# Empty edge slots and fill edges of a graph kernel read rows spread over the tables

## The chip, the cores and the metric

The kernel runs on one NeuronCore of a Trainium2 chip. Its engines work side by side, each through a queue of its own: PE (TensorE, matrix products), DVE (VectorE), ACT (ScalarE), POOL (GpSimd, which here issues the gathers) and SP (SyncE, which issues plain DMAs). Sixteen DMA engines move data between HBM and the on-chip memory SBUF. The metric is the device time of the whole kernel in microseconds.

## The reference, cut to what matters

Four layers run one after the other over one graph of 6250 nodes with 128 features and 100000 edges sorted by destination, each followed by a residual and a layer norm. What they do per edge:

```
L0 (twice):  agg[dst] += dinv[src] * w * dinv[dst] * h[src]
L1 (gat):    e = leaky(u[src] + v[dst]); agg[dst] += softmax_over_dst(e) * x[src]
L2 (hgt):    e = q[dst] . k[type][src];  agg[dst] += softmax_over_dst(e) * v[type][src]
L3:          e = relu(V [h[src], h[dst]]) + D h[src] + E h[dst]
             out[src] += scale * xw[dst] * e          (sums by src, self loops added)
```

## The kernel before, in words

**Slots.** Nodes are cut into NT = 49 tiles of P = 128. The kernel sorts the edges on the chip: each node tile gets a whole number of columns of 128 slots, and what is left of its last column stays empty. There are SC = 832 columns, 106496 slots for 100000 edges. One lane of a column is one partition. Tiles come in the order of their number of columns, and the last node tile comes last, so all columns that no tile needs stand at the very end of the order. There is one such order by destination (the d order) and one by source (the s order).

**Fill edges.** The input is laid out as 128 by UC = 784 entries, 352 more than there are edges. These 352 have src = dst = PAD_NODE = 6271, a node row that no real node has, and are sorted with the others; they stand at the end of the last tile's columns.

**What a slot reads.** `d_rec` in HBM holds one record of four numbers (src, dst key, typed row, weight) for each slot of the d order. Before the edges are scattered into it, DVE sets a buffer `fill` to zero with the key field at 1e6 (L400, L401) and SP copies it over `d_rec` (L364). ACT writes the edges' records, `d_recs`, from the sorted inputs (L370), and POOL scatters them (L721). So a slot that no edge takes keeps src = 0 and typed row = 0, and a fill edge has row 6271. The columns `d_src` and `d_typed` are read back from `d_rec`. For the s order, the tail of the second convolution decodes `s_dst` from a placing done with matrix products (`decoded`, L1365 to L1397); there an empty slot comes out as row 0 as well (L1391), and `dec_i` holds 256 for an empty slot and 0 for others (L1384).

**The five passes.** Each goes over all 832 columns in 104 groups of 8. For each column POOL issues one indirect DMA that fetches 128 table rows, one for each lane, at the row numbers in that column:

- c1: table t0 by `d_src`, rows of 512 B (L757); c2: table t1, the same
- gat: table t2 by `d_src`, 544 B; hgt: table t3 by `d_typed`, 1024 B
- L3: table t4 by `s_dst`, 1536 B (L2750)

Four group buffers are in use in turns (in L3 two, halved). In c1 and c2 PE waits for a group's landing (`landed`) and then multiplies the rows into the sums (L796). In gat and hgt DVE waits for it and scores (L2209, L2222), while ACT spills the rows to HBM; the weighing runs 12 groups behind. In L3 DVE waits for four columns at a time (L2836). A stage begins only when the last one is finished on all engines (`new_stage`).

Of the kernel before, what the change touches and what calls it, by code (L numbers as in the profile page):

```python
# [9 lines left out]
ALU = mybir.AluOpType  # L10
ACT = mybir.ActivationFunctionType
# [6 lines left out]
P = 128  # L18
NT = -(-N // P)
NP = NT * P  # L20
# [4 lines left out]
EC = P  # L25
UC = 784
UG = UC // 8
FULL_ROWS = E // EC
TAIL = E - FULL_ROWS * EC
# [3 lines left out]
SC = GROUPS * JC  # L33
# [10 lines left out]
SX = SC + 8 * (RING - 1)  # L44
BIG = 1.0e30
PAD_KEY = 1.0e6
HALF = (P - 1) / 2
EPS = 1e-5
AW = 35584
assert SC >= (UC * EC + NT * (P - 1)) // P and FULL_ROWS < UC and NG * GT == NT and UG % 2 == 0  # L50


# [24 lines left out]
def bcast_last(ap, n):  # L77
    shape = list(ap.shape) + [n]
    return ap.unsqueeze(len(shape) - 1).to_broadcast(shape)
# [6 lines left out]
def build(nc, t, out):  # L86
    ctx = ExitStack()
    with ctx:
# [21 lines left out]
        iota_part = sb("iota_part", 1)  # L110
# [34 lines left out]
        l3_T = sb("l3_T", 6 * D)  # L145
        arena = sb("arena", AW)

# [39 lines left out]
        e_in = {}  # L187
# [134 lines left out]
        d_recs = part(UC * 4).rearrange("p (c r) -> p c r", r=4)  # L322
# [9 lines left out]
        def hots(ap, keys, n, count):  # L332
# [10 lines left out]
        fill = part(JC * 16 * 4)  # L343
# [5 lines left out]
        tile_ge = part(SC)  # L349
        iota_c = part(SC)  # L350
        iota_ci = part(SC).bitcast(I32)
        split, filled, fill_set, iota_done, nodes, free, hist_done, base_v, base_p = (sem("h_" + n) for n in (
            "split", "filled", "fill_set", "iota_done", "nodes", "free", "done", "base_v", "base_p"))
        s_counts, d_counts = bank(0, 8 * NT), bank(1, NT)
        SIZED, PICKS = 3, 3
        with nc.Block() as block:
# [9 lines left out]

            @block.scalar
            def _(act):
                for f, n in enumerate(("src", "dst", "typ", "wgt")):
                    nc.scalar.activation(d_recs[:, :, f], e_in[n], ACT.Copy)  # L370

            @block.vector
            def _(dve):
                step = Chain(dve, split)
# [6 lines left out]
                for key, h, lo16, hi16 in ((e_in["src"], hi_int[0], s_lo16, s_hi16), (e_in["dst"], hi_int[1], d_lo16, d_hi16)):  # L381

                    step(nc.vector.tensor_scalar(h, key, -HALF, 1.0 / P, ALU.add, ALU.mult))
                    step(nc.vector.tensor_copy(hi16[:, 0:UC], h))
# [12 lines left out]
                for a in range(2):  # L397
                    step(nc.vector.tensor_tensor(w_rest, w_rest if a else e_in["wgt"], w_part[:, a], ALU.subtract))
                    step(nc.vector.tensor_copy(w_part[:, a + 1], w_rest))
                step(nc.vector.memset(fill, 0.0))  # L400
                nc.vector.memset(fill.rearrange("p (c r) -> p c r", r=4)[:, :, 1], PAD_KEY).then_inc(fill_set, 1)  # L401
                dve.wait_ge(iota_done, 1)
                step(nc.vector.tensor_copy(iota_c, iota_ci))
                dve.wait_ge(hist_done, 1)
                step = Chain(dve, base_v)
                step(nc.vector.tensor_copy(counts, d_counts))
# [841 lines left out]
        NODES_AT = 6144  # L1248
# [59 lines left out]
        class SecondNodes:  # L1308
# [9 lines left out]
            TAIL = 2 * (DONE + 1)  # L1318
# [47 lines left out]

            def decoded(self, dve, i):

                step = Chain(dve, self.d_v, (0, 3, 5, 6, 7, 8, 10, 12, 13, 13, 13)[i])
                if i == 0:  # L1370
                    step(nc.vector.tensor_scalar(small[:, 0:NT], s_degree, 1.0, None, ALU.add))
                    for z in range(2):
                        step(nc.vector.tensor_copy(dec_b[:, z * Q_W:(z + 1) * Q_W], place_bank(1, z)))
                elif i == 1:
                    for z in range(2):
                        step(nc.vector.tensor_copy(dec_a[:, z * Q_W:(z + 1) * Q_W], place_bank(0, z)))
                elif i == 2:
                    step(nc.vector.tensor_scalar(dec_int, dec_b, -HALF, 1.0 / P, ALU.add, ALU.mult))
                elif i == 3:
                    step(nc.vector.tensor_copy(dec_h, dec_int))  # L1380
                elif i == 4:
                    step(nc.vector.scalar_tensor_tensor(dec_b, dec_h, -float(P), dec_b, ALU.mult, ALU.add))
                elif i == 5:
                    step(nc.vector.tensor_scalar(dec_i, dec_a, 0.5, float(2 * P), ALU.is_lt, ALU.mult))  # L1384
                    step(nc.vector.tensor_tensor(s_lo[:, 0:SC], dec_b, dec_i, ALU.add))
                elif i == 6:
                    dve.wait_ge(self.d_deg, 1)
                    step(nc.vector.tensor_copy(deg_T, ps[0:NT, 3072:3072 + P]))
                    step(nc.vector.tensor_scalar(dec_a, dec_a, -1.0, 8.0, ALU.add, ALU.mult))
                elif i == 7:  # L1390
                    step(nc.vector.scalar_tensor_tensor(s_dst[:, 0:SC], dec_a, 0.0, dec_h, ALU.max, ALU.add))  # L1391
                elif i == 8:
                    dve.wait_ge(self.d_up, 1)
                    nc.vector.tensor_copy(dec_T.rearrange("p j e -> p (j e)"), ps[:, 2048:2048 + 7 * P]).then_inc(self.d_sb, 1)
                elif i == 9:
                    dve.wait_ge(self.d_deg, 2)
                    nc.vector.tensor_copy(inv[:, :], ps[:, 3584:3584 + NT])  # L1397
# [112 lines left out]
            def tensor_tail(self, pe):  # L1510
                for s in range(self.TAIL, self.TAIL + self.STEPS):
                    self.tensor_step(pe, s, self.in_tail(s, (0, 1, 2, 7, 8, 9)))
                    if s == self.TAIL + 4:
                        pe.wait_ge(self.d_v, 5)
                        nc.tensor.transpose(ps[0:NT, 3072:3072 + P], small[:, 0:NT], ident[:, :]).then_inc(self.d_deg, 1)
                        nc.tensor.matmul(ps[:, 2048 + 6 * P:2048 + 7 * P], ident[:, :], ident[:, :], start=True, stop=True)
                    if s == self.TAIL + 6:
                        pe.wait_ge(self.d_v, 10)
                        for j, k in BLOCKS:
                            last = nc.tensor.transpose(ps[0:k, 2048 + j * P:2048 + (j + 1) * P], s_lo[:, j * P:j * P + k], ident[:, :])  # L1520
                        last.then_inc(self.d_up, 1)
                    if s == self.TAIL + 7:
                        pe.wait_ge(self.d_v, 11)
                        nc.tensor.matmul(ps[:, 3584:3584 + NT], deg_T, rank_hot, start=True, stop=True).then_inc(self.d_deg, 1)

            def tensor_step(self, pe, s, todo):
# [38 lines left out]
        dec_a, dec_b, dec_h, dec_i = (arena[:, i * SC:(i + 1) * SC] for i in range(4))  # L1565
        dec_int = dec_i.bitcast(I32)
        dec_T = arena[:, 4 * SC:4 * SC + 7 * P].rearrange("p (j e) -> p j e", j=7)
        deg_T = arena[0:NT, 4 * SC + 7 * P:4 * SC + 8 * P]
        assert 4 * SC + 8 * P <= NODES_AT
        convolve("c1", t0, 0, FirstNodes)  # L1570
        convolve("c2", t1, 1, SecondNodes)

        class ThirdNodes:
# [8 lines left out]
            FIRST_HALF, TAIL, STEPS = 24, 2 * DONE, 5  # L1582
# [936 lines left out]
        r, x_new, summed_a = (scratch(AT_Q + i * GC, GC) for i in range(3))  # L2519
# [412 lines left out]
```

## Time and profile before

| | us |
|---|---|
| runs | 7548.39, 7556.19, 7559.97 (median 7556.19) |
| profiled execution | 7554.35, its span 7552.5 |
| POOL busy | 4883.0 (65%) |
| PE busy | 4910.9 (65%) |
| DVE busy | 4682.7 (62%) |
| ACT busy | 3188.4 (42%) |
| DMA | 925.24 MB, mean 123 GB/s |

No engine is busy all the time; the stages differ, and each has to be read by itself. The span leaves 1.85 us of the profiled execution outside. In the rows below, a row of the order of time gives start, duration, engine, line and operation; the brackets give the idle time of the engine just before it and what ended that.

### The profile page before, as it was taken

To read this page: it belongs to the slowest core of one execution; us is meant where nothing else is said; L and a number is where in the kernel's file an instruction comes from. 1 tells how busy PE (TensorE), PEld (TensorE's weight loads), DVE (VectorE), ACT (ScalarE), POOL (GpSimd) and SP (SyncE) were. 2 spreads that over 40 slices of the span, in tenths; PEclk is the share of its full clock that TensorE was granted. 3 is DMA by queue.
4 is the path that set the end of the run, shared out by engine and by line. 5 is a ranking of instruction groups with operands and counts; after the bars stand their busy time and mean duration, and the time that the engine had idled before them with its cause. 6 is when DMAs were issued, how large, how long until landed. Compare 5 with 4: busy or idle time off the path is not lost. (4 is left out here: it accounts for less than half of the span.)

```text
span 7552.5 us, 95692 instructions
## 1 busy us (share of the span) xinstructions
PE 4910.9 (65%) x26906; PEld 3728.8 (49%) x26906; DVE 4682.7 (62%) x12437; ACT 3188.4 (42%) x7393; POOL 4883.0 (65%) x4968
## 2 busy tenths in 40 slices
PE   8999801666676777774365655856656666777774
PEld 6777601444444455553254544435555543555553
DVE  8999801555554577775456666645666566566666
ACT  0222200444443444442244444746665642555553
POOL 0677775777776777774777773047777700777774
PEclk9776655888887888886566666967887787899997
DMA  1333201222223222223666665567777822766665
GB/s 29 79 82 79 58 2 28 52 55 55 56 55 48 53 56 55 56 55 56 168 180 183 183 183 118 195 196 230 231 230 224 221 69 82 217 209 210 209 208 146
DMA packets 817681, 925.24 MB, mean 123 GB/s; under 512 B 120147, under 2 KB 656219, under 8 KB 816923
## 3 DMA queue, kind: packets, MB, share of 16 engines
q0 software_dynamic: 198144, 441.54, 23.4%
q1 hardware_dynamic: 395118, 365.43, 16.2%
q10 hardware_dynamic: 223916, 112.15, 5.1%
q8 instruction: 245, 4.01, 0.2%
q14 instruction: 258, 2.11, 0.1%
HBM read 724.85 MB, written 193.87 MB: 122 GB/s over the span
## 5 line engine op out<-in xcount | busy, mean ns | idle before, releaser
L757 POOL DMA_INDIRECT arena<-t,d_src x2496 | 2441.0, 978 | 902.6 <-issue 759.2
L796 PE MATMUL ps<-arena 128*128 128x128 f32 (+2 forms) x8320 | 1779.4, 374 | 755.9 <-DMA arena<-t,d_src 623.5
L796 PEld LDWEIGHTS ps<-arena 128*128 128x128 f32 x8320 | 1567.2, 255 | 1015.7 <-issue 921.6
L805 DVE TENSOR_TENSOR arena<-arena,ps 128x512 f32 (+2 forms) x1040 | 835.4, 803 | 710.4 <-PE ps L796 656.9
L757 POOL DMA_INDIRECT arena<-t,d_typed x832 | 817.2, 982 | 488.8 <-issue 252.7
L721 POOL DMA_INDIRECT d_rec<-arena x784 | 789.0, 1006 | 442.7 <-issue 251.9
L2750 POOL DMA_INDIRECT arena<-t,s_dst x832 | 795.5, 956 | 295.6 <-issue 250.7
L793 PE MATMUL ps<-int_tmp 128*128 128x512 bf16 (+1 forms) x1664 | 554.7, 402 | 475.0 <-DVE arena L805 238.9
L1234 PE MATMUL ps<-arena 128*128 128x416 f16 x3328 | 770.4, 385 | 0.0
L1975 PE MATMUL ps<-arena 128*128 x2496 | 408.5, 296 | 451.7 <-ACT arena L1870 294.2
L1173 ACT ACTIVATE arena<-arena 128x128 f16<-128x128 f16 x1664 | 662.6, 480 | 6.9
L1975 PEld LDWEIGHTS ps<-arena 128*128 128x128 f32 (+1 forms) x2496 | 352.4, 204 | 518.9 <-issue 493.3
L1875 ACT ACTIVATE arena<-iota_row,d_lw 128x128 f32<-128x128 f32 x1664 | 506.5, 387 | 211.6 <-DMA arena<-t,d_src 167.6
L1193 DVE TENSOR_SCALAR arena<-iota_row,d_lw 128x128 f32<-128x128 f32 x1664 | 473.2, 360 | 79.4 <-DVE x_cur L1425 31.9
L1234 PEld LDWEIGHTS ps<-arena 128*128 128x128 f16 x3328 | 334.8, 114 | 249.7 <-issue 103.0
L1168 ACT ACTIVATE arena<-iota_row,arena 128x128 f16<-128x128 f32 x832 | 264.5, 391 | 426.3 <-PE ps L1236 409.5
L793 PEld LDWEIGHTS ps<-int_tmp 128*128 128x128 bf16 x1664 | 154.4, 110 | 581.6 <-DVE arena L805 308.8
L2779 ACT ACTIVATE arena<-iota_row,s_lo 128x128 f32<-128x128 f32 x832 | 254.4, 388 | 430.3 <-PE ps L796 430.3
L2836 DVE TENSOR_TENSOR ps<-ps,arena 128x512 f32<-128x512 f32 x208 | 145.3, 699 | 423.8 <-DMA arena<-t,s_dst 369.8
L2222 DVE TENSOR_TENSOR arena<-ps,arena 128x512 f32<-128x512 f32 x208 | 135.2, 687 | 404.0 <-DMA arena<-t,d_typed 357.6
L1202 DVE TENSOR_SCALAR arena<-arena 128x832 f16<-128x832 f16 x832 | 316.8, 442 | 0.0
L683 PEld LDWEIGHTS ps<-arena 128*128 128x128 f32 x1568 | 258.8, 254 | 53.1 <-issue 45.3
(451 smaller groups left out, 8054.2 us busy)
## 6 DMA issues: line engine op xcount, KB each, us to landing
spill<-arena ACTq DMA_DIRECT2D x208, 512.0 KB, 4.2
arena<-spill SPq DMA_DIRECT2D x208, 512.0 KB, 5.1
arena<-d_loT SPq DMA_DIRECT2D x208, 256.0 KB, 5.0
arena<-s_loT SPq DMA_DIRECT2D x104, 512.0 KB, 4.9
arena<-key_d SPq DMA_DIRECT2D x98, 512.0 KB
t<-arena SPq DMA_DIRECT2D x49, 1024.0 KB, 4.4
arena<-t,d_src POOLq DMA_INDIRECT x2496
arena<-t,d_typed POOLq DMA_INDIRECT x832
```

What stands on the lines that cost most here:

```text
L721: pool.indirect_dma_start(out=d_rec[:, :], out_offset=bass.IndirectOffsetOnAxis(ap=row[:, c:c + 1], axis=0), in_=d_recs[:, c, :], in_offse ...
L757: pool.indirect_dma_start(out=rows[r][:, i, :], out_offset=None, in_=table, in_offset=bass.IndirectOffsetOnAxis(ap=idx[:, 8 * n + i:8 * n ...
L793: nc.tensor.matmul(half[:, :, 0:self.width], zeros16[:, 0:P], self.blank, start=True, stop=False, skip_group_check=True)
L796: return nc.tensor.matmul(self.banks[i // 4][:, bass.ds(self.slot[i], self.width)], weights, rows, start=False, stop=False, skip_group_che ...
L805: nc.vector.tensor_tensor(at, at, got, ALU.add).then_inc(self.added, 1)
L1173: last = nc.scalar.activation(at_r[:, b, a, j], far[:, b, j], ACT.Relu, bias=places[:, 2 + 2 * a, at_c + j:at_c + j + 1], scale=places[:, ...
L1193: one_hot = nc.vector.tensor_scalar(at[:, s, :], iota_row[:, :], lw[:, 8 * n + i, 0:1], lw[:, 8 * n + i, 1:2], ALU.is_equal, ALU.mult)
L1202: nc.vector.tensor_scalar(at_q[:, b, j], iota_q, places[:, 0, at_c + j:at_c + j + 1], None, ALU.is_equal)
L1234: nc.tensor.matmul(place_bank(a, z), at_r[:, b, a, j], at_q[:, b, j, z * Q_W:(z + 1) * Q_W], start=False, stop=False, skip_group_check=True)
L1875: last = nc.scalar.activation(at[:, b, i], iota_row[:, :], ACT.Abs, bias=lw[:, 8 * n + i, 0:1], scale=-1.0)
L1975: last = nc.tensor.matmul(looked_up(b, z)[:, (i - 4 * z) * tab_w:(i - 4 * z + 1) * tab_w], hot_T[:, b, i * P:(i + 1) * P], source[:, bass. ...
L2750: pool.indirect_dma_start(out=rows[:, 8 * b + i, :], out_offset=None, in_=t4, in_offset=bass.IndirectOffsetOnAxis(ap=s_dst[:, 8 * n + i:8 ...
```

## The change

An empty slot and a fill edge are given row numbers that differ from slot to slot. In the d order, the empty record's src and typed row become 7 times the slot's position modulo 832 (0 to 5817); the fill edges' src and typed row become 49 times their lane (0 to 6223). In the s order an empty slot's row becomes 49 times its lane; the fill edges' `s_dst` stays at 6271. The keys stay, so where an edge goes and what is summed stay too.

```diff
+SPREAD, LANE_SPREAD = 7, 49
@@ first sorting stage, ACT
+                for f in (0, 2):
+                    nc.scalar.activation(d_recs[:, FULL_ROWS:UC, f], iota_part[:, 0:1].to_broadcast([P, UC - FULL_ROWS]), ACT.Copy, scale=float(LANE_SPREAD)).then_inc(pads_set, 1)
                 for f, n in enumerate(("src", "dst", "typ", "wgt")):
-                    nc.scalar.activation(d_recs[:, :, f], e_in[n], ACT.Copy)
+                    if n in ("src", "typ"):
+                        nc.scalar.activation(d_recs[:, 0:FULL_ROWS, f], e_in[n][:, 0:FULL_ROWS], ACT.Copy)
+                        act.wait_ge(pads_set, 2)
+                        nc.scalar.activation(d_recs[0:TAIL, FULL_ROWS, f:f + 1], e_in[n][0:TAIL, FULL_ROWS:FULL_ROWS + 1], ACT.Copy)
+                    else:
+                        nc.scalar.activation(d_recs[:, :, f], e_in[n], ACT.Copy)
@@ first sorting stage, DVE
-                step(nc.vector.memset(fill, 0.0))
-                nc.vector.memset(fill.rearrange("p (c r) -> p c r", r=4)[:, :, 1], PAD_KEY).then_inc(fill_set, 1)
                 dve.wait_ge(iota_done, 1)
                 step(nc.vector.tensor_copy(iota_c, iota_ci))
+                fields = fill.rearrange("p (c r) -> p c r", r=4)
+                step(nc.vector.memset(fill, 0.0))
+                step(nc.vector.memset(fields[:, :, 1], PAD_KEY))
+                nc.vector.tensor_scalar(fields[:, :, 0:4:2], bcast_last(iota_c, 2), float(SPREAD), None, ALU.mult).then_inc(fill_set, 1)
@@ tail of the second convolution, DVE (the counts of d_v that others wait for go up by one or two)
                 if i == 0:
                     step(nc.vector.tensor_scalar(small[:, 0:NT], s_degree, 1.0, None, ALU.add))
+                    step(nc.vector.tensor_scalar(spread, iota_part[:, 0:1], LANE_SPREAD / (2 * P), None, ALU.mult))
@@
                 elif i == 7:
+                    step(nc.vector.scalar_tensor_tensor(dec_h, dec_i, spread, dec_h, ALU.mult, ALU.add))
                     step(nc.vector.scalar_tensor_tensor(s_dst[:, 0:SC], dec_a, 0.0, dec_h, ALU.max, ALU.add))
```

On DVE, in the first sorting stage, before (L400 and L401 set `fill`, L403 makes `iota_c`, L406 reads the first counts):

```order
L399 CAST arena<-arena 128x784
L400 MEMSET arena 128x3328
L401 MEMSET arena 128x832
L403 CAST arena<-arena 128x832
L406 COPY arena<-ps 128x49
```

and now:

```order
L408 CAST arena<-arena 128x784
L410 CAST arena<-arena 128x832
L412 MEMSET arena 128x3328
L413 MEMSET arena 128x832
L414 TENSOR_SCALAR arena<-arena 128x1664
L417 COPY arena<-ps 128x49
```

The making of `iota_c` stands ahead of the two memsets now, and a TENSOR_SCALAR over 1664 elements stands behind them, ahead of the counts.

On DVE, in the tail of the second convolution, the last steps of the decoding, before:

```order
L1450 TENSOR_SCALAR arena<-x_cur,arena 128x128 x4
L1465 TENSOR_TENSOR arena<-arena,bias_sb 128x512
L1466 TENSOR_TENSOR arena<-arena,bias_sb 128x512
L1391 SCALAR_TENSOR_TENSOR s_dst<-arena 128x832
L1394 COPY arena<-ps 128x896
```

and now:

```order
L1463 TENSOR_SCALAR arena<-x_cur,arena 128x128 x4
L1478 TENSOR_TENSOR arena<-arena,bias_sb 128x512
L1479 TENSOR_TENSOR arena<-arena,bias_sb 128x512
L1403 SCALAR_TENSOR_TENSOR arena<-arena 128x832
L1404 SCALAR_TENSOR_TENSOR s_dst<-arena 128x832
L1407 COPY arena<-ps 128x896
```

One more pass over 832 elements stands directly ahead of the one that writes `s_dst`.

## Rows read from the trace of the kernel before

**Rows 1.** the costliest groups: line, engine, operation, count | busy us, mean ns | idle, releasers

```profile
L757 POOL DMA_INDIRECT arena<-t,d_src x2496 | 2441.0, 978 | 902.6 <-issue 759.2
...
L2750 POOL DMA_INDIRECT arena<-t,s_dst x832 | 795.5, 956 | 295.6 <-issue 250.7
```

**Rows 2.** stretches: us; PE, PEld, DVE, ACT, POOL busy (instructions); PEclk, DMA share, GB/s

```profile
2320.00:2360.00 40.00, 26.89 (x152) 18.48 (x152) 21.91 (x66) 18.98 (x52) 30.56 (x32) 0.87 0.22 57
2376.00:2404.00 28.00, 16.30 (x78) 12.07 (x79) 9.70 (x28) 4.46 (x12) 12.05 (x13) 0.74 0.85 36
5980.00:6010.00 30.00, 16.62 (x103) 14.83 (x102) 21.72 (x40) 14.13 (x33) 23.30 (x23) 0.73 0.71 212
6033.00:6061.00 28.00, 12.69 (x72) 11.70 (x72) 10.05 (x16) 12.37 (x25) 10.70 (x11) 0.68 1.00 109
```

**Rows 3.** order of time, end of c1, POOL and PE

```profile
2350.07 0.94 POOL L757 DMA_INDIRECT arena<-t,d_src  x1 [0.30 <-issue]
...
2352.66 1.15 PE L796 MATMUL ps<-arena 128*128 128x128 f32 x8 [3.02 <-DMA arena<-t,d_src]
...
2389.86 2.07 PE L796 MATMUL ps<-arena 128*128 128x128 f32 x8 [5.46 <-DMA arena<-t,d_src]
...
2390.76 0.94 POOL L757 DMA_INDIRECT arena<-t,d_src  x1 [0.30 <-issue]
...
2403.57 1.64 PE L796 MATMUL ps<-arena 128*128 128x128 f32 x6 [5.70 <-DMA arena<-t,d_src]
```

**Rows 4.** order of time, end of c2, POOL and PE

```profile
3479.81 0.95 POOL L757 DMA_INDIRECT arena<-t,d_src  x1 [0.30 <-issue]
...
3492.06 2.07 PE L796 MATMUL ps<-arena 128*128 128x128 f32 x8 [4.39 <-DMA arena<-t,d_src]
```

**Rows 5.** order of time, end of gat, POOL and DVE

```profile
4588.47 0.94 POOL L757 DMA_INDIRECT arena<-t,d_src  x1 [0.30 <-issue]
...
4592.18 0.36 DVE L2209 TENSOR_REDUCE arena<-ps 128x64 f32<-128x192 f32 x1 [6.40 <-DMA arena<-t,d_src]
...
4619.44 0.95 POOL L757 DMA_INDIRECT arena<-t,d_src  x1 [0.30 <-issue]
...
4637.06 0.36 DVE L2209 TENSOR_REDUCE arena<-ps 128x64 f32<-128x192 f32 x1 [6.30 <-DMA arena<-t,d_src]
```

**Rows 6.** order of time, end of hgt, POOL and DVE

```profile
5985.20 0.95 POOL L757 DMA_INDIRECT arena<-t,d_typed  x1 [0.30 <-issue]
...
5989.94 1.29 DVE L2222 TENSOR_TENSOR arena<-ps,arena 128x512 f32<-128x512 f32 x2 [3.38 <-DMA arena<-t,d_typed]
...
6045.92 0.95 POOL L757 DMA_INDIRECT arena<-t,d_typed  x1 [0.30 <-issue]
...
6063.61 1.29 DVE L2222 TENSOR_TENSOR arena<-ps,arena 128x512 f32<-128x512 f32 x2 [8.75 <-DMA arena<-t,d_typed]
```

**Rows 7.** order of time, end of L3's pass, POOL and DVE

```profile
7438.86 0.96 POOL L2750 DMA_INDIRECT arena<-t,s_dst  x1 [0.30 <-issue]
...
7442.28 0.70 DVE L2836 TENSOR_TENSOR ps<-ps,arena 128x512 f32<-128x512 f32 x1 [0.51 <-DMA arena<-t,s_dst]
...
7469.10 0.96 POOL L2750 DMA_INDIRECT arena<-t,s_dst  x1 [0.30 <-issue]
...
7481.90 0.70 DVE L2836 TENSOR_TENSOR ps<-ps,arena 128x512 f32<-128x512 f32 x1 [3.47 <-DMA arena<-t,s_dst]
```

**Rows 8.** order of time, first sorting stage and the next one's start, DVE and ACT

```profile
173.52 0.75 DVE L401 MEMSET arena<- 128x832 f32 x1 [0.83 <-DVE arena L400]
...
200.97 0.92 ACT L560 ACTIVATE arena<-arena 128x392 bf16<-128x392 bf16 x1 [168.65 <-DVE arena L334]
```

**Rows 9.** order of time, tail of c2, DVE

```profile
3529.24 0.59 DVE L1389 TENSOR_SCALAR arena<-arena 128x832 f32<-128x832 f32 x1
...
3533.38 1.02 DVE L1391 SCALAR_TENSOR_TENSOR s_dst<-arena 128x832 int32<-128x832 f32 x1
...
3538.91 0.69 DVE L1472 TENSOR_TENSOR arena<-ps,bias_sb 128x512 f32<-128x512 f32 x1 [3.38 <-PE ps L1543]
```

More of the change, by code:

```diff
@@ L49 @@
 AW = 35584
+assert SPREAD * (SC - 1) < NP and LANE_SPREAD * (P - 1) < NP and EC == P and TAIL % 32 == 0
 assert SC >= (UC * EC + NT * (P - 1)) // P and FULL_ROWS < UC and NG * GT == NT and UG % 2 == 0
@@ L351, in build @@
         iota_ci = part(SC).bitcast(I32)
-        split, filled, fill_set, iota_done, nodes, free, hist_done, base_v, base_p = (sem("h_" + n) for n in (
-            "split", "filled", "fill_set", "iota_done", "nodes", "free", "done", "base_v", "base_p"))
+        split, filled, fill_set, pads_set, iota_done, nodes, free, hist_done, base_v, base_p = (sem("h_" + n) for n in (
+            "split", "filled", "fill_set", "pads_set", "iota_done", "nodes", "free", "done", "base_v", "base_p"))
         s_counts, d_counts = bank(0, 8 * NT), bank(1, NT)
@@ L1367, in decoded @@
             def decoded(self, dve, i):
-                step = Chain(dve, self.d_v, (0, 3, 5, 6, 7, 8, 10, 12, 13, 13, 13)[i])
+                step = Chain(dve, self.d_v, (0, 4, 6, 7, 8, 9, 11, 13, 15, 15, 15)[i])
                 if i == 0:
                     step(nc.vector.tensor_scalar(small[:, 0:NT], s_degree, 1.0, None, ALU.add))
+                    step(nc.vector.tensor_scalar(spread, iota_part[:, 0:1], LANE_SPREAD / (2 * P), None, ALU.mult))
                     for z in range(2):
@@ L1513, in tensor_tail @@
                     if s == self.TAIL + 4:
-                        pe.wait_ge(self.d_v, 5)
+                        pe.wait_ge(self.d_v, 6)
                         nc.tensor.transpose(ps[0:NT, 3072:3072 + P], small[:, 0:NT], ident[:, :]).then_inc(self.d_deg, 1)
@@ L1517, in tensor_tail @@
                     if s == self.TAIL + 6:
-                        pe.wait_ge(self.d_v, 10)
+                        pe.wait_ge(self.d_v, 11)
                         for j, k in BLOCKS:
@@ L1522, in tensor_tail @@
                     if s == self.TAIL + 7:
-                        pe.wait_ge(self.d_v, 11)
+                        pe.wait_ge(self.d_v, 12)
                         nc.tensor.matmul(ps[:, 3584:3584 + NT], deg_T, rank_hot, start=True, stop=True).then_inc(self.d_deg, 1)
@@ L1568, in build @@
         deg_T = arena[0:NT, 4 * SC + 7 * P:4 * SC + 8 * P]
-        assert 4 * SC + 8 * P <= NODES_AT
+        spread = arena[:, 4 * SC + 8 * P:4 * SC + 8 * P + 1]
+        assert 4 * SC + 8 * P + 1 <= NODES_AT
         convolve("c1", t0, 0, FirstNodes)
```

## The prediction, made before the changed kernel ran

> **What bounds the kernel now.** I read the costliest groups first. POOL issues 832 gathers in each of five passes; one takes about 0.98 us and 0.3 us of idle time that the profile puts down to nothing but issue [rows 1]. So a pass lasts at least 832 columns by some 1.27 us, and inside a pass PE or DVE wait for landings, never the reverse: POOL's idle time ahead of a gather is 0.30 us to the last one [rows 3 to 7]. The change takes no gather away, so it can't shorten this part.
>
> The second view is the table of stretches, for what the DMA engines do near the end of a pass [rows 2]. In c1 they are busy 22% and move 57 GB/s from 2320 to 2360 us. From 2376 to 2404 they are busy 85% and move only 36 GB/s. In hgt they go from 71% and 212 GB/s to 100% and 109 GB/s. More time for fewer bytes: in these last microseconds each row has become dear. The input says which columns those are. Counted from the reference's inputs, the d order fills 809 of 832 columns and the s order 810, so the last 23 (22) are empty and all their 128 lanes read row 0; the 352 fill edges before them are 2.75 columns that all read row 6271.
>
> The third view is the order of time there. Gathers go in groups of 8, group 99 (columns 792 to 799) being the last before the fill edges and group 103 the last of all. In c1 group 99's last issue ends at 2350.07 + 0.94 = 2351.01 and PE starts on it at 2352.66, 1.65 us later; group 103's ends at 2391.70 and PE starts at 2403.57, 11.87 us later [rows 3]. The last two groups land 2403.57 - 2389.86 = 13.71 us apart, 1.71 us for a column or 13.4 ns for a row, where POOL takes (2390.76 - 2350.07) / 32 = 1.27 us for a column. A column of one row is thus slower to fetch than to issue, by 0.44 us; 25.75 such columns make 11.4 us, near the measured growth of 11.87 - 1.65 = 10.22. After this last landing come only products, sums and stores, then the next stage: this lag is on the path.
>
> **The change part by part.**
>
> *The lag at the end of each pass.* It goes if spread rows are fetched faster than POOL issues them, as random rows are in mid-pass at 22% (c1) or 71% (hgt) of the DMA engines [rows 2]. I take the wait of a normal group for the wait that stays.
> - c1: 11.87 - 1.65 = 10.2 us [rows 3].
> - c2: last issue ends 3480.76, PE starts 3492.06: 11.3; the table has the same row size, so c1's normal 1.65 holds: 9.7 us [rows 4].
> - gat: last issue ends 4620.39, DVE scores at 4637.06: 16.7. Group 100 took 4592.18 - 4589.41 = 2.8 [rows 5], with two columns of fill edges in it; taken as normal, 13.9 us. With c1's 1.65 it would be 15.0.
> - hgt: 6063.61 - 6046.87 = 16.7, normal 5989.94 - 5986.15 = 3.8: 12.9 us [rows 6].
> - L3: 7481.90 - 7470.06 = 11.8, normal 7442.28 - 7439.82 = 2.5, for half groups: 9.3 us [rows 7]. Its fill edges keep row 6271; 2.75 columns by 0.4 us are 1.2 us of lag, which the 22 columns behind them make up.
>
> The sum is 56.0 us. Is each on the path? PE waited 5.7 us for c1's last landing and 4.4 for c2's [rows 3, 4]; of c1's 13.71 us between landings, 8.0 were work, and that fits into POOL's 10.2 us for a group. In gat and hgt DVE idled 6.3 and 8.8 us ahead of the last score, so it keeps up too, also if landings come 3 or 4 us closer together; behind it the weighing of 12 groups follows in program order, no sooner and no later than before [rows 5, 6]. In L3 DVE idled 3.5 us ahead of the last four columns [rows 7].
>
> *Empty slots inside used columns.* Each tile's last column has on average 65 of them. At 13.4 ns they cost 0.87 us, under the 1.27 us of issue, so they delay nothing that POOL's pace doesn't cover: zero, now and after.
>
> *First sorting stage, DVE.* A TENSOR_SCALAR of 1664 elements is added on DVE's chain: `iota_c` and the counts follow one on the other, without a wait for another engine. 832 elements took 0.59 us in that operation and 1.02 us in one with two inputs [rows 9]; twice as many lie between 1.0 and 1.9 us (estimates by doubling less the fixed part). The second memset is now waited for, and behind such a wait stood 0.83 us [rows 8]; between 0 and 0.8. Sum +1.0 to +2.7, I take +2.0. The copy of `fill` starts as much later, and hides: the stage ends at about 200 us, 26 us behind the memset [rows 8].
> By the Trainium skill (VectorE: DVE Perf Modes, Mode 2×_2P) an fp32 operation with one tensor input can run at two elements a cycle. The 0.59 us row agrees. With it this addition would be at the low end, and the forecast 1 us lower, which a measurement of this kernel can't show.
>
> *First sorting stage, ACT.* Two small ACTIVATEs and two tails of one column come in. ACT's next work after this stage follows 168.65 us of idle time [rows 8]: zero. Without that cover they would cost some 1 us.
>
> *Tail of c2, DVE.* The pass over 832 elements ahead of `s_dst` takes 1.02 us like its neighbour [rows 9]. DVE idles 3.38 us for PE shortly behind it, which covers it: zero, 1.0 if not. The small operation for `spread` is on the chain there, +0.2.
>
> The sum: -56.0 + 2.0 + 0.2 = -53.8 us. On the profiled execution, 7554.35, that gives 7500.5; it lay 1.8 us under the median of the runs, 7556.19, so the median should be **7502**.
>
> **The rivals.**
>
> *Spread rows are served only half better.* The new rows aren't random: 7 rows apart from lane to lane in the d order, 49 apart in the s order, and there the same 128 rows in all 22 columns. If a column then takes 1.5 us in place of 1.71, half of the lag stays: 7556 - 28 + 2 = 7530. Against it: the same DMA engines serve random rows in a fraction of the time. For it: no row of before shows a regular step. 12%.
>
> *The gain in gat and hgt meets the next limit.* If PE, DVE or the spill's way out and back takes over half of their 26.8 us: 7502 + 13 = 7515. For it: the DMA engines are at 71% there in mid-pass, and the weighing waits for reloads. Against: the idle times above. 12%.
>
> *Not the row.* The lag might come from something else at a pass's end, and the spreading then does nothing: 7556 + 2 = 7558. Against it: issue, size and count of the gathers are the same in group 99 and group 103; what differs is what the row numbers say. 5%.
>
> *Slower.* A regular step could send all lanes to one part of the memory and be worse than one row. The place is the same last 22 to 23 columns. Were a column to take 3.4 us, twice today's, the lag of a pass would be (3.4 - 1.27) by 23 = 49 us in place of 10, and five passes would add about 195 us: 7750. It is slower than before once a column takes over 1.71 us, and by over 0.2% from about 1.84 (15 us over five passes of 23 columns). Nothing in the trace speaks for it. 3%.
> The Trainium skill (DMA: Bandwidth & Descriptors, Latency and other measured facts) has such a loss, to half the rate, for HBM row pitches of large powers of two up to several MiB. [...]
>
> **How the numbers follow.** Chances: forecast 68% (7488 to 7520), half served 12%, next limit 12%, not the row 5%, slower 3%. If no lag at all were left, the sum would be -68 + 2, or 7490, so 7488 is the low end, with a microsecond or two for the runs' own scatter. The high end takes in the half-served case: 7530. That leaves out about 1 in 10 and the tails. About 0.2%, 15 us, is what a measurement of this kernel can tell from no change: faster needs under 7541, which the first three cases give, less a little for a poorly served one: 89%. Within 0.2%: 8%. Slower: 3%.
>
> **What would show it.** In the changed profile: the last PE start of c1 and c2 1.5 to 3 us behind POOL's last issue, DVE's last score 2 to 5 us behind it in gat and hgt, and 2 to 4 in L3; DMA share in the last 28 us of c1 near 22%, not 85%; each pass's POOL time unchanged; the first sorting stage 1 to 3 us longer. The prediction is wrong if landings in the last group still come 13 us apart, or if they come at POOL's pace and the stage ends no sooner.

## The result, and the profile after

| | us |
|---|---|
| before, runs beside it | median 7554.81 (7546.55 to 7559.97, 6 runs) |
| changed kernel | median 7495.75 (7485.98 to 7500.12, 6 runs) |
| ratio | 0.9922, 95% interval 0.9909 to 0.9935 |
| profiled execution | 7495.48, its span 7493.7 |

The change saves 59 us, 0.8%. The span of the profiled execution fell by 58.8, from 7552.5. (Two sets of later runs were some 16% slower for every kernel, the one before included; their totals are compared only within their set, and they are called runs at the slow pace.)

First the stretches, as in [rows 2]. Columns: us; busy time of PE, PEld, DVE, ACT, POOL with instruction counts; PE's granted clock; DMA share; GB/s. Here c1's last 28 us are 2367 to 2395.

```profile
2320.00:2360.00 40.00, 27.14 (x147) 19.18 (x146) 20.65 (x63) 18.66 (x50) 30.53 (x31) 0.84 0.21 55
2367.00:2395.00 28.00, 20.87 (x112) 14.48 (x110) 15.44 (x44) 9.82 (x27) 21.29 (x23) 0.82 0.19 51
...
6000.00:6020.00 20.00, 11.37 (x73) 10.23 (x71) 10.64 (x17) 13.12 (x32) 10.67 (x11) 0.82 0.66 196
```

The end of c1 now looks like its middle. The DMA engines are busy 19% where they were busy 85%, and move 51 GB/s where they moved 36. In hgt 66% and 196 GB/s stand against 100% and 109.

Then the order of time at the ends of the passes, which answers to [rows 3 to 7]. c1:

```profile
2386.93 1.19 PE L807 MATMUL ps<-arena 128*128 128x128 f32 x8 [3.09 <-DMA arena<-t,d_src]
...
2394.51 0.94 POOL L768 DMA_INDIRECT arena<-t,d_src  x1 [0.30 <-issue]
...
2397.10 1.15 PE L807 MATMUL ps<-arena 128*128 128x128 f32 x8 [3.03 <-DMA arena<-t,d_src]
...
2410.17 0.94 POOL L768 DMA_INDIRECT arena<-t,d_src  x1 [14.71 <-POOLq L103]
```

POOL's last issue ends at 2395.45 and PE starts on that group at 2397.10, 1.65 us later, exactly what a normal group took before [rows 3]; it was 11.87. The last two groups start 10.17 us apart, which is POOL's pace for 8 columns, no longer 13.71. The next pass's first gather waits 14.71 us; in the trace of before that bracket is 25.51.

c2, gat, hgt and L3:

```profile
3473.26 0.94 POOL L768 DMA_INDIRECT arena<-t,d_src  x1 [0.30 <-issue]
...
3475.89 1.29 PE L807 MATMUL ps<-arena 128*128 128x128 f32 x8 [2.87 <-DMA arena<-t,d_src]
```

```profile
4601.78 0.95 POOL L768 DMA_INDIRECT arena<-t,d_src  x1 [0.30 <-issue]
...
4605.94 0.36 DVE L2223 TENSOR_REDUCE arena<-ps 128x64 f32<-128x192 f32 x1 [3.76 <-DMA arena<-t,d_src]
...
6012.76 0.95 POOL L768 DMA_INDIRECT arena<-t,d_typed  x1 [0.30 <-issue]
...
6015.59 1.29 DVE L2236 TENSOR_TENSOR arena<-ps,arena 128x512 f32<-128x512 f32 x2 [4.90 <-DMA arena<-t,d_typed]
...
7419.08 0.70 DVE L2850 TENSOR_TENSOR ps<-ps,arena 128x512 f32<-128x512 f32 x1 [1.94 <-DMA arena<-t,s_dst]
...
7420.98 0.96 POOL L2764 DMA_INDIRECT arena<-t,s_dst  x1 [0.30 <-issue]
...
7424.10 0.70 DVE L2850 TENSOR_TENSOR ps<-ps,arena 128x512 f32<-128x512 f32 x1 [1.86 <-DMA arena<-t,s_dst]
```

The lags are 1.7, 3.2, 1.9 and 2.2 us where they were 11.3, 16.7, 16.7 and 11.8. POOL's pace is what it was: its groups of gathers have the same mean and the same idle time for issue as in [rows 1], and only the idle time between passes is less (881.1 where 902.6 stood, for the three passes by `d_src`):

```profile
L768 POOL DMA_INDIRECT arena<-t,d_src x2496 | 2441.7, 978 | 881.1 <-issue 759.5 <-POOLq L103 121.7
```

Here is where the span went. The table cuts it into the five passes, each from POOL's first gather to the end of its last issue, and the gaps between, from the start and end times of those rows:

| us | before | after | difference |
|---|---|---|---|
| start to c1's first gather | 1325.52 | 1328.83 | +3.31 |
| the five passes, issue time | 5327.85 | 5326.56 | -1.29 |
| gap behind c1 | 25.51 | 14.71 | -10.80 |
| gap behind c2 | 68.54 | 58.07 | -10.47 |
| gap behind gat | 356.03 | 342.20 | -13.83 |
| gap behind hgt | 366.61 | 351.56 | -15.05 |
| from L3's last issue to the end | 82.49 | 71.74 | -10.75 |

The five gaps give 60.9 us; with the other two rows 58.9, the whole change of the span.

### The profile page after: what moved, and what is told of

It reads as the page before. It is cut to its first block and busy times, and to the rows that moved or that the text cites. A ratio compares the mean times of both kernels' runs of the same rounds, so it can differ in the third digit from the quotient of the medians.

```text
span 7493.7 us, 95699 instructions
## 1 busy us (share of the span) xinstructions
PE 4880.7 (65%) x26906; PEld 3706.3 (49%) x26906; DVE 4683.1 (62%) x12440; ACT 3189.1 (43%) x7397; POOL 4882.0 (65%) x4968
## 5 line engine op out<-in xcount | busy, mean ns | idle before, releaser
L768 POOL DMA_INDIRECT arena<-t,d_src x2496 | 2441.7, 978 | 881.1 <-issue 759.5
```

The lines of the kernel that those rows point to most:

```text
L768: pool.indirect_dma_start(out=rows[r][:, i, :], out_offset=None, in_=table, in_offset=bass.IndirectOffsetOnAxis(ap=idx[:, 8 * n + i:8 * n ...
```

## Experiments

The first four ran side by side (before: 7570.64, the median of 25 runs). The gaps given with them are of their profiled executions.

**Zero steps.** The changed kernel with all its instructions and both steps at 0: does the gain come from the row numbers?

```diff
-SPREAD, LANE_SPREAD = 7, 49
+SPREAD, LANE_SPREAD = 0, 0
```

> The changed kernel with both steps set to 0: every instruction of the change is there, but empty slots and fill edges read row 0 again. Theory (the row numbers alone make the gain): the end of c1 lags again by 10 us (PE starts 11.9 us behind POOL's last issue, not 1.65), the gap between POOL's last gather of a pass and the first of the next is that of the kernel before in all four places (25.5, 68.5, 356 and 367 us, within 1), and the whole takes what the kernel before takes plus 1 to 3 us, so a ratio of 1.0001 to 1.0004. Rival (the moved steps or where they stand make part of the gain): the ratio is clearly under 1, near 0.992 if all of it.

Measured: 7573.68, ratio 1.0006 (0.9996 to 1.0015). Every gap is back (26.85, 70.86, 356.71, 368.99, 83.02 us), though three of the first four are 1.3 to 2.4 us longer than before's, where within 1 was expected. The end of c1 in its trace:

```profile
2390.01 0.94 POOL L768 DMA_INDIRECT arena<-t,d_src  x1 [0.30 <-issue]
2390.45 2.07 PE L807 MATMUL ps<-arena 128*128 128x128 f32 x8 [6.22 <-DMA arena<-t,d_src]
...
2403.98 2.07 PE L807 MATMUL ps<-arena 128*128 128x128 f32 x8 [6.38 <-DMA arena<-t,d_src]
```

The lag is 2403.98 - 2390.95 = 13.0 us, and the groups are again 13.5 us apart. The row numbers alone make the whole gain; the added instructions cost nothing that can be measured. The lag is 1.2 us longer than before's 11.87. What differs from before is that the fill edges now read row 0 too, not a row of their own; that is also the likely reason for the longer gaps.

**The d order alone, the s order alone.** In the first the step of the decoding is 0; in the second `SPREAD` and the step of the fill edges are.

```diff
-  step(nc.vector.tensor_scalar(spread, iota_part[:, 0:1], LANE_SPREAD / (2 * P), None, ALU.mult))
+  step(nc.vector.tensor_scalar(spread, iota_part[:, 0:1], 0.0, None, ALU.mult))
```

> Rows are spread in the d order alone (passes c1, c2, gat, hgt); an empty slot of the s order reads row 0, since the decoding multiplies by 0. Theory: each pass carries its own lag, so L3's comes back in full (about 10 us) and the four others stay away: 7496 + 10 = 7506 us, ratio 0.9935. DVE's last landing in L3 again 11.8 us behind POOL's last issue. Rival (the lags hang together, an earlier pass's end feeds the next): L3's lag differs from 11.8 us by over 1 us.

Measured: 7514.63, ratio 0.9931 (0.9915 to 0.9948), some 52 us, where 0.9935 was expected. Four gaps are within 1.2 us of those of after (14.39, 58.28, 342.68, 350.43), and L3's is that of before, 82.68. Its last gather and score show the 11.75 us:

```profile
7413.07 0.96 POOL L2764 DMA_INDIRECT arena<-t,s_dst  x1 [0.30 <-issue]
7419.07 0.70 DVE L2850 TENSOR_TENSOR ps<-ps,arena 128x512 f32<-128x512 f32 x1 [3.57 <-DMA arena<-t,s_dst]
7425.78 0.70 DVE L2850 TENSOR_TENSOR ps<-ps,arena 128x512 f32<-128x512 f32 x1 [3.55 <-DMA arena<-t,s_dst]
```

The last two scores, each of which waited for its four columns, are 6.71 us apart here, 1.68 a column; in the changed kernel 5.02, 1.26.

```diff
-SPREAD, LANE_SPREAD = 7, 49
+SPREAD, LANE_SPREAD = 0, 49
-  nc.scalar.activation(d_recs[:, FULL_ROWS:UC, f], ..., ACT.Copy, scale=float(LANE_SPREAD))
+  nc.scalar.activation(d_recs[:, FULL_ROWS:UC, f], ..., ACT.Copy, scale=0.0)
```

> Rows are spread in the s order alone (pass L3); empty slots and fill edges of the d order read row 0. Theory: L3's gain alone, about 10 us, less 1 to 3 us of added steps: 7548 us, ratio 0.9990. The four gaps of the d passes are as in the kernel before within 1 us. Rival: with spread rows at L3's place alone the gain is near 0, since something else takes over there.

Measured: 7566.52, ratio 0.9996 (0.9986 to 1.0005). L3's last gap is 71.43, 11.1 us less than before, and the last score follows 2.1 us behind the last issue, as in the changed kernel. But the other four gaps are longer than before's by 1.3, 2.3, 0.5 and 3.0 us, where within 1 was expected. The first experiment has the same, and in both the d order's fill edges read row 0. 7.1 of the 11.1 us are lost so and 4.0 remain; the medians differ by 4.1, but the interval of the ratio takes in 1, so the total shows no gain by itself. The expected ratio was 0.9990. That each order's spreading acts on its own passes is shown; the total is not a clean sum of parts, because what the fill edges read moves it.

**Fill edges alone.** They keep their spread rows, all empty slots read row 0: how much of the lag is the fill edges'?

```diff
-SPREAD, LANE_SPREAD = 7, 49
+SPREAD, LANE_SPREAD = 0, 49
-  step(nc.vector.tensor_scalar(spread, iota_part[:, 0:1], LANE_SPREAD / (2 * P), None, ALU.mult))
+  step(nc.vector.tensor_scalar(spread, iota_part[:, 0:1], 0.0, None, ALU.mult))
```

> Only the 352 fill edges of the d order are spread (2.75 columns); the 23 empty columns behind them read row 0, in both orders. Theory (each column of one row adds its own 0.44 us of lag): each d pass ends 1.2 us earlier than with all in one row, so PE starts 10.7 us behind POOL's last issue in c1 in place of 11.9, and the whole gains some 5 us less the added 1 to 3: about 7552. Rival (the fill edges alone start a jam that the empty columns only carry on): over 3 us less lag in each pass.

Measured: 7570.95, ratio 1.0002 (0.9991 to 1.0012).

```profile
2405.59 2.07 PE L807 MATMUL ps<-arena 128*128 128x128 f32 x8 [5.94 <-DMA arena<-t,d_src]
...
2419.61 0.95 POOL L768 DMA_INDIRECT arena<-t,d_src  x1 [25.72 <-POOLq L103]
```

The last issue ended at 2419.61 - 25.72 = 2393.89, so c1's lag is 11.70 us, before's within 0.2. The expected 1.2 us less did not come. So there are three cases of c1's lag: fill edges on row 0 with the empty slots, 13.03; on a row of their own, 11.87; spread, 11.70. Only the first adds to the lag. By the price of 0.44 us a column over POOL's pace, 23 columns make 10.1 us and 25.75 make 11.3; above the normal 1.65 the trace has 10.2 in before and 11.4 with zero steps. Columns of another row add nothing to the lag at the end, then, where columns of row 0 follow. The next runs ask what makes a row dear.

**One row, two rows, many rows, in a whole pass.** Three kernels made from the one before, at the slow pace (before there: 8722.16, a single run). The columns of `d_src`, `d_typed` and `s_dst` are not used as row numbers; each pass reads for all its columns one fixed column `pick`, row number lane // (128 / k) * step. `PICKS_OF` gives k (how many different rows) and step for c1, c2, gat, hgt and L3, in this order for the first, second and third kernel. So the sums are not the reference's; sizes, counts and issue are.

```diff
-  in_offset=bass.IndirectOffsetOnAxis(ap=idx[:, 8 * n + i:8 * n + i + 1], axis=0)
+  in_offset=bass.IndirectOffsetOnAxis(ap=pick[:, gather_pass[0] - 1:gather_pass[0]], axis=0)
+PICKS_OF = [(1, 0), (2, 1), (4, 1), (1, 0), (1, 0)]
+PICKS_OF = [(8, 1), (2, 1000), (1, 0), (2, 1), (2, 1)]
+PICKS_OF = [(128, 1), (128, 32), (128, 49), (128, 256), (128, 1)]
```

> The kernel before, but every gather of a pass reads a fixed set of rows, in place of its edges' rows (so the results mean nothing): in c1 all 128 lanes read row 0; in c2 half of the lanes row 0 and half row 1; in gat four neighbouring rows, 32 lanes each; in hgt and L3 row 0 for all. Theory (fetches of one row are served one after the other at some 13.4 ns, whatever its size up to 1536 B): c1 takes 832 x 1.71 = 1423 us from first to last landing where it took 1078; hgt 832 x 1.75 = about 1460; L3 832 x 1.66 = about 1380. In c2 with two rows, if the rows are served side by side, 0.86 us for a column, under POOL's 1.27: c2 as before (1064 us of issue), and gat too. Rival (it is the number of bytes or the pass's end that matters): c1 stays at 1066. Second rival (neighbouring rows share what is slow): c2 is as slow as c1.

> As the run with fixed rows in every pass: in c1 eight neighbouring rows of 512 B, 16 lanes each; in c2 two rows 1000 apart (512000 B); in gat row 0 (544 B) for all; in hgt rows 0 and 1 (1024 B); in L3 rows 0 and 1 (1536 B). Theory: c1 at POOL's pace, 1066 us; c2 with two rows at POOL's pace like its neighbouring pair in the other run; gat 832 x 1.75 = about 1460 us; hgt and L3 at POOL's pace (1070 and 1057) if two rows are served side by side. Rival (what is shared is a larger piece of memory than a row): two neighbouring rows are as slow as one, two distant rows are not.

> As the runs with fixed rows in every pass, but 128 different rows: in c1 neighbours (512 B apart), in c2 32 rows apart (16 KiB), in gat 49 rows apart (26656 B), in hgt 256 rows apart (256 KiB), in L3 neighbours (1536 B apart). Theory (different rows, whatever their step, are served faster than POOL issues): all five at POOL's pace, 1066, 1064, 1071, 1070 and 1057 us of issue. Rival (a step of a power of two sends all lanes to one part of the memory, up to half the rate or worse): c2 or hgt longer by over 5%, hgt most.

Measured: 9475.19, 9052.18 and 8739.78 (a single run each). Stretches inside c1, hgt and L3 of the three kernels, and inside gat of the last two; columns: us, POOL busy with its instructions, PE's clock, DMA share, GB/s. The first kernel (one row in c1, four in gat, one in hgt, one in L3):

```profile
1700.00:2500.00 800.00, 456.97 (x476) 0.75 0.92 42
...
6100.00:6900.00 800.00, 386.32 (x392) 0.67 0.94 143
8100.00:8600.00 500.00, 272.63 (x286) 0.80 0.99 150
```

The second (eight rows, one, two, two):

```profile
1700.00:2500.00 800.00, 537.91 (x554) 0.74 0.17 49
...
4500.00:5300.00 800.00, 396.08 (x405) 0.60 0.97 118
6100.00:6900.00 800.00, 467.30 (x474) 0.69 0.61 170
8100.00:8600.00 500.00, 330.00 (x346) 0.82 0.56 182
```

The third (128 rows in each):

```profile
1700.00:2500.00 800.00, 535.14 (x552) 0.73 0.17 49
...
4500.00:5300.00 800.00, 477.60 (x487) 0.63 0.51 143
6100.00:6900.00 800.00, 475.15 (x478) 0.70 0.60 176
8100.00:8600.00 500.00, 330.92 (x346) 0.80 0.60 182
```

Read the gathers in a stretch: with one row 476, 405, 392 and 286; with two or more 552 to 554, 485 to 487, 474 to 478 and 346. With one row the DMA engines are busy 92 to 99%, otherwise 17 to 61%. Two rows in a column are enough, next to each other or, in c2, 1000 rows apart (546 gathers in 800 us both times, 545 with 128 rows). More rows gain little on two: in hgt the issue of the whole pass took 1398.3 us with two rows and 1372.7 with 128, 2% less, and L3 took 1203.8 both times. A step of 32 rows in c2 (16 KiB) and of 256 rows in hgt (256 KiB) costs nothing: in c2 the DMA engines are busy 16%, where neighbouring rows in c1 have 17%. This takes away the rival in which a regular step would be slow, for these two steps.

One limit of these runs: at the slow pace a column of c1 and c2 takes 1.46 us and not 1.27, so that two rows keep up with POOL's normal pace isn't shown by them; the last experiment takes that up. They also show that it is not the bytes that make a row dear: one row of 544 B in gat took 1652.9 us for the pass, 1.99 a column, and one row of 1024 B in hgt 1662.7, 2.00. Both passes have the spill beside them.

**Empty slots alone, and the change again.** Is the fill edges' part worth anything? The first of the pair leaves out all that the change does to `d_recs` on ACT; the second is the changed kernel. Both ran at the slow pace (before there: 8777.33, 19 runs).

```diff
-  for f in (0, 2):
-      nc.scalar.activation(d_recs[:, FULL_ROWS:UC, f], iota_part[:, 0:1].to_broadcast(...), ACT.Copy, scale=float(LANE_SPREAD)).then_inc(pads_set, 1)
...
+      nc.scalar.activation(d_recs[:, :, f], e_in[n], ACT.Copy)
```

> The change without its ACT part: empty slots are spread in both orders, the 352 fill edges keep row 6271. Theory (the empty columns at the very end make the lag; what the fill edges' 2.75 columns add is made up behind them): the same time as the whole change, within 0.1% of it, about 7496 on a chip where the kernel before takes 7555, ratio 0.992; the ends of c1 and c2 lag as in the changed kernel, within 0.3 us. Rival (each column of one row adds its own 0.44 us for good, as my sum of 25.75 columns had it): 1.2 us more in each of four passes, so 5 us slower than the whole change.

> The changed kernel again, beside the one without the fill edges' part and on the same chip. Both theories: ratio 0.992 to the kernel before. It is there to say how much of a difference between the two is their own, and whether the 2.7 us by which the stages before c1 were longer in its first profile come back (if they do, the added steps cost more than the 0.6 us read at the first sorting stage; if not, they were scatter).

Measured: 8759.58, ratio 0.9987 (0.9967 to 1.0008), and 8782.78, ratio 0.9996 (0.9979 to 1.0014). Neither differs from before here, and the pair tells nothing of the fill edges. That the change itself gains nothing here was not expected. The trace of the second kernel shows who sets the pace. PE's products with the rows, in the changed kernel at the normal pace and in this run:

```profile
L807 PE MATMUL ps<-arena 128*128 128x128 f32 (+2 forms) x8320 | 1762.7, 372 | 743.6 <-DMA arena<-t,d_src 611.7
```

```profile
L807 PE MATMUL ps<-arena 128*128 128x128 f32 (+2 forms) x8320 | 1782.7, 365 | 445.3 <-issue 388.1
```

One product takes as long as ever (365 ns, 372). But where PE idled for landings, it now idles between products for nothing that the profile shows. In c1 it waits for a landing twice, where it did so 104 times at the normal pace; DVE in gat and hgt does so at most twice, where it was 88 and 80 times. Only in L3 does DVE still wait for landings, up to the last one. The end of c1:

```profile
2692.51 0.37 PE L807 MATMUL ps<-arena 128*128 128x128 f32 x1 [1.80 <-issue]
...
2697.74 0.94 POOL L768 DMA_INDIRECT arena<-t,d_src  x1 [0.30 <-issue]
...
2710.47 1.05 PE L807 MATMUL ps<-arena 128*128 128x128 f32 x8
```

PE takes up the last group 11.8 us behind POOL's last issue, with no wait ahead of it, although no row is dear in this kernel: it is still busy with earlier groups. POOL waits for buffers in turn, and c1's issue takes 1214.3 us, 1.46 a column. Rows that land 10 us late would find PE busy there, so that the lag of c1 and c2, and likewise that of gat and hgt, would be hidden; L3's 10 us are 0.1%, which the interval still allows. This is argued from the changed kernel alone: no profile of the kernel before was taken at that pace. What PE's added idle times are is open.

**One row a column.** Are two rows served side by side when they stand in different gathers? Again fixed columns in place of the row numbers, so the sums are not the reference's. c1: row 0 always. c2 and hgt: columns of row 0 and of row 1 in turns. L3: groups of eight columns of row 0 and of row 1000 in turns. gat: 128 rows, step 49. At the slow pace, beside the pair above.

```diff
+        def chosen(which, n, i):
+            c = (0, (0, 1)[i % 2], 3, (0, 1)[i % 2], (0, 2)[n % 2])[which]
+            return pick[:, c:c + 1]
-  in_offset=bass.IndirectOffsetOnAxis(ap=idx[:, 8 * n + i:8 * n + i + 1], axis=0)
+  in_offset=bass.IndirectOffsetOnAxis(ap=chosen(gather_pass[0] - 1, n, i), axis=0)
```

> The kernel before with fixed rows for every gather (the results mean nothing): c1 reads row 0 in all lanes of all columns; c2 and hgt read row 0 in even columns and row 1 in odd ones, all 128 lanes of a column the same row; gat reads 128 rows, 49 apart; L3 reads row 0 for the 8 columns of a group and row 1000 for the next 8. Theory (one row's fetches queue up behind each other, two rows are served side by side, also if they belong to different gathers in flight): c2 goes at POOL's pace like gat, c1 at 1.13 or more times POOL's pace, hgt at the pace it had with two rows. Rival (a gather is slow when its own 128 rows are one): c2 and hgt as slow as c1 with one row. L3: by the theory as slow as one row where only one group is in flight, between the two if several are.

Measured: 8960.43 (a single run).

```profile
1700.00:2500.00 800.00, 457.92 (x476) 0.75 0.97 42
3100.00:3900.00 800.00, 523.16 (x540) 0.79 0.44 48
...
6100.00:6900.00 800.00, 475.44 (x477) 0.69 0.69 177
8100.00:8600.00 500.00, 328.54 (x344) 0.85 0.89 180
```

With row 0 always, 476 gathers in 800 us; with two rows in turns 540, 477 and (in 500 us) 344, where the changed kernel beside it has 540, 478 and 342. So two rows are served side by side also from different gathers, even where eight columns of the one follow eight of the other. That fits the fill edges on row 6271, which added nothing to the lag at the end: their columns could be fetched beside those of row 0.

**Empty slots alone, once more,** at the normal pace (before: 7551.14, 7 runs); the edit is that of the pair.

> The change without its ACT part once more, since the first comparison ran where every kernel took 16% longer and told nothing. Theory (the fill edges' 2.75 columns are made up behind them): as the whole change, ratio 0.992, ends of c1 and c2 within 0.3 us of the changed kernel's (PE's last rows 2.98 and 3.20 us behind POOL). Rival (each column of one row counts for good): 1.2 us more lag in each of four passes, 0.993.

Measured: 7490.8, ratio 0.9922 (0.9905 to 0.9938), the ratio of the whole change. The gaps are those of after (14.76, 58.23, 341.70, 349.84, 71.65), and PE starts on the last group 1.60 (c1) and 1.73 us (c2) behind POOL's last issue, within 0.3 us of after's 1.65 and 1.69, as expected. The spreading of the d order's fill edges contributes nothing that can be measured. They have a lag of their own, though. Group 100, which holds most of their columns, and the next one, in c1:

```profile
2355.82 0.94 POOL L761 DMA_INDIRECT arena<-t,d_src  x1 [0.30 <-issue]
...
2359.68 2.07 PE L800 MATMUL ps<-arena 128*128 128x128 f32 x8 [4.28 <-DMA arena<-t,d_src]
...
2366.07 0.94 POOL L761 DMA_INDIRECT arena<-t,d_src  x1 [0.30 <-issue]
...
2368.62 1.33 PE L800 MATMUL ps<-arena 128*128 128x128 f32 x8 [2.06 <-DMA arena<-t,d_src]
```

PE starts on group 100 2.92 us behind its last issue and on group 101 1.61 us behind: 1.3 us of lag, made up within one group.

**One row at the normal pace.** Row 0 in every column of c1, hgt and L3; c2 in turns; gat 128 rows. Is the price of a one-row column the same when POOL is quicker?

```diff
-            c = (0, (0, 1)[i % 2], 3, (0, 1)[i % 2], (0, 2)[n % 2])[which]
+            c = (0, (0, 1)[i % 2], 3, 0, 0)[which]
```

> The kernel before with fixed rows for every gather (the results mean nothing): c1 (512 B rows), hgt (1024 B) and L3 (1536 B) read row 0 for every lane of every column; c2 reads row 0 in even and row 1 in odd columns, gat 128 rows 49 apart. Theory (12.8 to 13.4 ns for each fetch of one row, whatever its size): c1 issues for 1362 to 1423 us where it took 1066, L3 for 1380 to 1452 where it took 1057, c2 and gat at POOL's pace (1064, 1071). hgt took 2.0 us a column where the chip was slower: between 1.7 and 2.0, 1420 to 1660. Rival (the 16% slower chip made its own price): a price clearly under 12.8 ns here.

Measured: 8838.18 (a single run). Stretches in c1, c2, hgt and L3, columns as in [rows 2]:

```profile
1500.00:2500.00 1000.00, 568.47 (x2840) 423.47 (x2839) 422.26 (x1235) 342.12 (x925) 574.64 (x599) 0.75 1.00 42
2800.00:3800.00 1000.00, 739.70 (x4199) 546.57 (x4198) 745.06 (x2583) 477.90 (x1425) 763.32 (x777) 0.83 0.51 55
5400.00:6400.00 1000.00, 410.38 (x2306) 371.82 (x2306) 378.69 (x658) 376.72 (x758) 487.95 (x496) 0.68 0.98 144
7600.00:8600.00 1000.00, 645.30 (x2560) 469.07 (x2558) 443.04 (x568) 411.64 (x782) 544.30 (x571) 0.80 0.88 150
```

From its first gather to its last issue c1 takes 1361.49 us, where the first fixed-row kernel took 1361.28 at the slow pace. So the price belongs to the fetching, not to the issue. Per column it is 1.64 us in c1 (512 B rows), 1.98 in hgt (1024 B, with the spill beside it) and 1.75 in L3 (1536 B), from issue times of 1361.5, 1651.5 and 1453.8: 12.8, 15.5 and 13.7 ns a row. The expected price, 12.8 to 13.4 ns, holds for c1 and nearly for L3; hgt's 1651.5 us is inside its own expected range. c2, in turns, runs near POOL's pace, 1070.3 us against before's 1063.5; the other profiles at this pace have 1063.3 to 1065.1, so one row a column in turns costs some 6 us here. And POOL now waits inside c1, for buffers that PE hands on late.

## Why the prediction was right, point by point

**The bound.** POOL's pace held: 5326.6 us of issue in five passes against 5327.8. Nothing inside a pass got faster.

**The lag.** The forecast took 56.0 us off the five lags; the gaps shrank by 60.9. c1 was to give 10.2 and gave 10.8, c2 9.7 and 10.5, gat 13.9 and 13.8, hgt 12.9 and 15.1, L3 9.3 and 10.8. "The wait of a normal group is the wait that stays" was exact in c1 and c2 (1.65 and 1.69), near in gat (3.2 for 2.8) and L3 (2.2 for 2.5), and mis-sized in hgt: 1.9 for 3.8. That one term is 2 of the 5 us that were missed; 3 more stand behind the lag.

**What stands behind the lag.** The forecast let products, sums and stores after the last landing be as they were. They got shorter. From PE's last start behind a landing to the next pass's first gather, the four profiles at the normal pace that have the lag in c1 took 13.6 to 14.0 us, and the three without it 12.8 to 13.2; for c2 it is 57.0 to 57.9 against 56.4 to 56.6. From L3's last score to the end it is 70.6 to 71.4 against 69.4 to 69.6. That is 0.6, 0.9 and 1.1 us between before and after; in gat and hgt the difference is 0.4 and 0.2, inside the scatter. PE's clock goes with it. Before, PE had idled 5.70 us ahead of c1's last group and 5.46 ahead of the one before it [rows 3], and in 4 us around the start of the last group its granted clock was 0.50, which is 1.2 GHz. In the changed kernel it had idled 3.03 and was granted 0.77 there. Columns as in [rows 2]; first before, then after:

```profile
2403.00:2407.00 4.00, 3.43 (x15) 3.29 (x16) 0.69 (x1) 0.00 (x0) 0.00 (x0) 0.50 0.00 0
```

```profile
2396.00:2400.00 4.00, 2.90 (x17) 2.81 (x18) 0.69 (x1) 0.00 (x0) 0.00 (x0) 0.77 0.06 16
```

The first eight products of the last group take 1.15 us and not 2.07 (the last row of [rows 3] shows six of its eight, because that view ends there). In L3 the last eight products, for which the last sum waits, take 1.99 us where they took 3.27, more than the 1.1 us found there; first before, then after:

```profile
7485.20 3.27 PE L796 MATMUL ps<-arena 128*128 128x256 f32 x8 [0.38 <-DVE arena L2843]
```

```profile
7427.39 1.99 PE L807 MATMUL ps<-arena 128*128 128x256 f32 x8 [0.81 <-DVE arena L2857]
```

The shortening is shown to come with the shorter lag; that the clock is all of it is argued, and no run has separated it.

**The count of dear columns.** The step that reached 11.4 us from 25.75 columns, "near the measured" 10.22, was wrong in its count, and nearness hid it. 23 columns make 10.1. The fill edges' 2.75 columns add to the lag at the end only if they read the same row as the rest: zero steps had 11.4 over the normal, before 10.2. The sum did not use this figure, so the forecast wasn't harmed. The sentence on L3, by which fill edges that keep row 6271 lag by 1.2 us that the columns behind make up, is borne out in c1 by the last run of empty slots alone: 1.3 us of lag, gone one group later.

**First sorting stage.** DVE, with the memset, the added operation and the next stage's first row, as in [rows 8]:

```profile
173.64 0.75 DVE L413 MEMSET arena<- 128x832 f32 x1 [0.83 <-DVE arena L412]
174.43 1.03 DVE L414 TENSOR_SCALAR arena<-arena 128x1664 f32<-128x1664 f32 x1
...
201.58 0.92 ACT L571 ACTIVATE arena<-arena 128x392 bf16<-128x392 bf16 x1 [169.37 <-DVE arena L336]
```

The next stage's ACT row starts at 201.58, 0.6 us later than the 200.97 of [rows 8], where 2.0 was taken and 1.0 to 2.7 was the range. The operation cost 1.03, its low end, and starts 0.04 us behind the second memset. The wait of 0.83 us behind the memset of 3328 elements had been there before [rows 8], so no such wait was added.
The Trainium skill (VectorE: DVE Perf Modes, Mode 2×_2P) has two elements a cycle for such an operation, and the trace agrees: 1664 elements took 1.03 us, as long as 832 elements in the operation with two inputs (1.02 in [rows 9]), although the output is written in steps of two.
c1's first gather comes 3.3 us later than before. In the first four experiments, which have the same operations, it comes at 1322.84 to 1328.11 (1325.31 with zero steps), against before's 1325.52, so most of the 3.3 is scatter of the sorting stages, not the change's cost.

**Tail of c2.** The added pass took 1.08 us (at 3516.39), and DVE's idle time for PE behind it fell from the 3.38 of [rows 9] to 2.01. It is hidden, as forecast.

**The rivals.** "Not the row" fell to the zero steps. "Half served" fell to landings 10.17 us apart in c1. "The next limit" fell to gaps that shrank by 13.8 and 15.1 in gat and hgt. "Slower" fell to the same landings with the change's own steps, and the fixed rows add that steps of 16 KiB and of 256 KiB run at the pace of other rows.
The Trainium skill (DMA: Bandwidth & Descriptors, Latency and other measured facts) gives its loss for DMA copies of 16 KiB a partition, at row pitches of 512 KiB and more. For gathered rows of 512 and 1024 B no loss was seen at these two steps, which lie below the page's; whether gathers have the loss at its pitches, no run shows.

Together: 4.9 us too little from the lags, 1.6 too much for the two places on DVE (2.2 taken, 0.6 measured), and -1.3 and +2.7 us of the passes and of the sorting stages that are scatter. The span fell by 58.8 where 53.8 was forecast. The path and the cause were right. What was off are the size of hgt's normal wait, the 3 us behind the lags that were put at nothing, and the size of the sorting stage.

## What to carry to other kernels

Where slots of a gather hold nothing, don't let them all name one row. Before you spread them, look for a stretch in which DMA share rises while GB/s falls, and compare what a one-row gather takes to land with what it takes to issue: only the excess, times the number of such gathers in a row, can be gained, and only if no other work hides it: at the slow pace PE was behind the landings anyway, and the change gained nothing that could be measured. Two distinct rows were nearly enough here, in one gather or in neighbouring ones.

## What the runs showed of the hardware

- Fetches of one row cost what they would if they went by one at a time: 12.8 ns each at 512 B and 13.7 at 1536 B. Beside the spill traffic it is 15.5, both at 544 B (gat) and at 1024 B (hgt). Three times the bytes cost 7% more, so it is mostly a price per fetch. All 16 DMA engines show as busy the while (1.00 at 42 GB/s), so a high DMA share doesn't mean that much is moved. Whether the row is held up in HBM or in how the DMA engines ask for it is open.
- A second row is served beside the first. With two rows in turns c2's DMA share is 0.51 at 55 GB/s; with the edges' rows (the changed kernel's c1) it is 0.21 at the same 55 GB/s. So two rows are still dearer than many, but the pass took only 1070.3 us in place of 1063.5.
- At the slow pace each kernel took some 16% longer. One instruction took as long as always (PE's products 365 ns, 372 at the normal pace), and PE idled between them, 1.80 us in the row shown, for nothing that the profile shows. What that is is open.
